# Reordering the products and the output parts in layer 0's attention loop of a two-layer gated cross-attention kernel

## The reference, cut to what matters

```python
# x: (8, 128, 512) float32, ctx_4096: (8, 128, 512), D=512, 32 heads of 128
x = x + jnp.tanh(g_xattn[0]) * _L0_xattn_ref(_layernorm(x), ctx_4096, mask, bias, ln_w, w_q, w_k, w_v, w_out)
x = x + jnp.tanh(g_ffn[0])   * _L0_ffn_ref(_layernorm(x), qweight, lut4, lut8, bias)      # dequantised weight
x = x + jnp.tanh(g_xattn[1]) * _L1_xattn_ref(_layernorm(x), ctx_4096, Wq, Wk, Wv, Wo, q_norm_w, k_norm_w)
x = x + jnp.tanh(g_ffn[1])   * _L1_ffn_ref(_layernorm(x), weight, bias)

# _L0_xattn_ref, with x = rmsnorm(hidden) * ln_w:
h_q = (x @ w_q.T); h_k = (kv @ w_k.T); h_v = (kv @ w_v.T)        # each split into 32 heads
score = softmax(where(mask, h_q h_k^T + bias, -inf)); score = where(mask, score, 0)
attn = score h_v                                                 # (b, q, 32*128)
out = attn @ w_out.T
return hidden_states + out
```

## Time and profile before

| | |
|---|---|
| median of 3 runs | 1681.61 us (1681.59 to 1682.12) |
| profiled execution, its own time | 1681.52 us |
| its span, first to last instruction | 1679.7 us |
| PE busy | 1663.4 us (99%) |
| DVE, ACT, POOL busy | 1190.1 (71%), 1001.6 (60%), 603.5 us (36%) |
| layer 0's loop | about 415.8 to 890 us of the span |

### The profile page before, as it was taken

One profiled execution on the slowest core, in us unless ns is written; L12 is line 12 of the kernel. 1 busy time (PEld: TensorE's weight loads), 2 busy tenths in 40 slices (PEclk: granted clock), 3 DMA queues, 4 the chain that ended last, 5 costly groups with the idle time before them and its releaser, 6 DMA issues.

```text
span 1679.7 us, 30969 instructions
## 1 busy us (share of the span) xinstructions
PE 1663.4 (99%) x10269; PEld 1477.9 (88%) x10269; DVE 1190.1 (71%) x2245; ACT 1001.6 (60%) x2540; POOL 603.5 (36%) x584
## 2 busy tenths in 40 slices
PE   9999999999999999999999999999999999999998
PEld 8899999999888888888888888888888888888887
DVE  6444446576787787777788877777676767677677
ACT  5344434345767777776776666656666665666563
POOL 2422223201434443534435543333333333333343
PEclk9999999999999999999999999999999999999999
DMA  6444444544233333333332110101010111111001
GB/s 227 175 167 157 150 150 150 192 165 161 95 106 102 112 112 99 126 100 120 108 113 83 39 51 24 63 26 59 12 62 25 52 32 50 36 36 41 14 7 51
DMA packets 80591, 153.31 MB, mean 91 GB/s; under 512 B 6544, under 2 KB 58128, under 8 KB 76944
## 3 DMA queue, kind: packets, MB, share of 16 engines
q1 hardware_dynamic: 80528, 152.50, 26.9%
HBM read 108.43 MB, written 44.04 MB: 91 GB/s over the span
## 4 chain that ended last, share of the span: by engine, by line
PE 87%; DVE 5%; ACT 3%; issue 3%; POOL 2%; DMA 1%; SPq 0%; ACTq 0%; POOLq 0%; DVEq 0%
PE bank L2103 20%; PE bank L2050 15%; PE bank L2052 15%; PE bank L2051 15%; PE bank L2280 7%; PE bank L2500 3%; PE bank L2238 3%; PE bank L2316 3%; PE bank L2400 2%; PE bank L2526 2%; PE bank L2226 1%; DMA vraw<-wv 1%; PE bank L2531 1%; ACT pr L1048 1%; PE bank L2072 0%
## 5 line engine op out<-in xcount | busy, mean ns | idle before, releaser
L2050 PE MATMUL bank<-w_hi,xt_hi 128*128 (+2 forms) x512 | 178.0, 348 | 1.2 <-DVE qt_lo L1949 1.1
L747 POOL TENSOR_TENSOR p<-p,rn 128x512 f32<-128x512 f32 x128 | 133.5, 1044 | 122.1 <-DVE rn L1917 118.8
L2052 PE MATMUL bank<-w_hi,xt_lo 128*128 (+2 forms) x512 | 172.7, 337 | 0.0
L2051 PE MATMUL bank<-w_lo,xt_hi 128*128 (+2 forms) x512 | 171.4, 335 | 0.0
L690 POOL TENSOR_TENSOR pr<-pr,rn 128x512 f32<-128x512 f32 x64 | 67.5, 1055 | 284.3 <-DVE rn L1564 284.3
L1203 ACT ACTIVATE p<-bank,nb,q_r 128x256 f32<-128x256 f32 x256 | 141.2, 562 | 3.3 <-DVE nb L1913 0.8
L609 POOL TENSOR_TENSOR q_r<-q_ms,half 128x4 f32<-128x4 f32 x64 | 64.4, 1007 | 190.6 <-DVE q_ms L1892 190.6
L1048 ACT ACTIVATE pr<-sc,nmax 128x128 f32<-128x128 f32 x256 | 99.9, 391 | 41.6 <-DVE nmax L1549 41.3
L609 POOL TENSOR_TENSOR k_r<-k_ms,half 128x2 f32<-128x2 f32 x64 | 59.3, 927 | 144.3 <-DVE k_ms L1871 144.3
L2050 PE MATMUL bank<-w_hi,ot_hi 128*128 (+1 forms) x256 | 106.2, 415 | 1.3 <-DVE ot_lo L1937 1.3
L2050 PEld LDWEIGHTS bank<-w_hi,xt_hi 128*128 128x128 f32 x512 | 96.2, 188 | 12.4 <-DVE qt_lo L1949 1.6
(11 more groups left out here) (293 smaller groups left out, 5605.2 us busy)
## 6 DMA issues: line engine op xcount, KB each, us to landing
stage<-w SPq DMA_DIRECT2D x35, 512.0 KB, 3.2
keys_of_layer<-kout SPq DMA_DIRECT2D x16, 1024.0 KB, 4.5
values_of_layer<-vout SPq DMA_DIRECT2D x16, 1024.0 KB, 5.2
kt<-keys_of_layer SPq DMA_DIRECT2D x64, 256.0 KB, 3.3
vs<-values_of_layer SPq DMA_DIRECT2D x64, 256.0 KB, 2.8
vraw<-wv SPq DMA_DIRECT2D x10, 1024.0 KB, 6.7
kraw<-wk SPq DMA_DIRECT2D x16, 512.0 KB, 5.6
stage0o<-w SPq DMA_DIRECT2D x16, 512.0 KB, 3.3
```

The costliest lines, as they stand in the source:

```text
L747: pool.tensor_tensor(p1[:, half_p:half_p + 2, :], p1[:, half_p:half_p + 2, :], rn1[:, half_p:half_p + 2].unsqueeze(2).to_broadcast([P, 2, ...
L2050: nc.tensor.matmul(out_ap, l_hi, r_hi, start=(c == 0), stop=False)
L2051: nc.tensor.matmul(out_ap, l_hi, r_lo, start=False, stop=False)
L2052: op = nc.tensor.matmul(out_ap, l_lo, r_hi, start=False, stop=(c == n - 1))
```

## The change

In layer 0's loop, from the last slot of turn 0 on:

- PE makes the output projection right behind the query products and the attention product at the end of the slot.
- ACT makes `output_hi` at the head of the next slot instead of late in its own.
- DVE makes `output_lo` at the head of the next slot, ahead of `maxima`, instead of behind `inverse_sums`.
- In turn 7, slots 4 to 7, PE's order stays; slot 4 now takes `output_hi` and `output_lo` at its head as slots 5 to 7 do already, and there DVE makes them ahead of `accumulate(i - 2)`.

No instruction is added or taken away.

```diff
--- before.py
+++ after.py
@@ -1067,8 +1067,7 @@
                 last = isinstance(t, int) and t == TL - 1
 
                 if last and j >= 4:
-                    if j > 4:
-                        output_hi(i - 1, j - 2)
+                    output_hi(i - 1, j - 2)
                     code_distance(t, j // 4, p, i + 1)
                     probabilities_copied(i)
                     code_mask(i + 1)
@@ -1078,6 +1077,8 @@
                     query_weight_late(n + 1)
                 if first and j == 1:
                     queries_out(3)
+                if not first:
+                    output_hi(i - 1, j - 2)
                 if not (first and j == 0):
                     probabilities_copied(i)
                 if first and j == 0:
@@ -1092,7 +1093,7 @@
                         queries_out(k + 1)
                 if not first:
                     query_part(n + 1, 1 - parity, p)
-                if not (first and j == 0):
+                if first and 0 < j < BODY - 1:
                     output_hi(i, j - 1)
                 if first and j == 3:
                     act.wait_ge(w_in[0], 48)
@@ -1689,10 +1690,9 @@
                 active = not first
 
                 if last and j >= 4:
+                    output_lo(i - 1, (j - 2) % 2)
                     if j == 4:
                         accumulate(i - 2, 2)
-                    else:
-                        output_lo(i - 1, (j - 2) % 2)
                     maxima(i + 1, j % 2)
                     if j == 4:
                         output_weight_lo(n, parity)
@@ -1719,7 +1721,7 @@
                 inverse_sums(i + 1, 2 * (j % 4))
                 if first and j == 1:
                     query_weight_lo(1, 2)
-                if lag1:
+                if first and 0 < j < BODY - 1:
                     output_lo(i, (j - 1) % 2)
                 if first:
                     behind_output(j)
@@ -2355,9 +2357,12 @@
                 if not (first and j == 0):
                     if not isinstance(t, int):
                         pe.wait_ge(v_in[(j - 1) % 2], 16 * (4 * t + (j + 1) // 2))
-                    attention_output(i, (j - 1) % 2)
+                    if first and j < BODY - 1:
+                        attention_output(i, (j - 1) % 2)
                 if not (first and j < 2):
                     output_projection(i - 1, (j - 2) % BODY, 2 * t + (j - 2) // 4)
+                if not (first and j < BODY - 1):
+                    attention_output(i, (j - 1) % 2)
 
             pe.wait_ge(c12_done, LAST_JOB)
             transpose_rows(0, 4)
```

## The result

| | before | after |
|---|---|---|
| median, five runs of each on one chip | 1681.75 us (1681.59 to 1682.81) | 1699.78 us (1695.98 to 1700.58) |
| ratio, with its 95% interval | | 1.0103 [1.0092, 1.0114] |
| profiled execution, its own time and span | 1681.52, 1679.7 | 1700.58, 1698.7 |

The change makes the kernel 1.0% slower.

The account below looks back on a forecast made before the run. The prediction took PE, busy 99% of the span, to bound the kernel. Its terms, 12.5 + 0.8 + 0.7 + 2.3 + 1.2 = 17.5 us on the profiled execution's 1681.5, gave 1699.0 us, range 1692.5 to 1704.5.

Parts of the forecast that it names:

- Term 1: Short slots: PE waits 0.90 us for YA's accumulation before the projection; 7.37 us against 6.36, over 13 slots +12.5.
- The head of turn 7: Slots 5 to 7 of turn 7, taken as model of the changed slot's head: accumulation starts 2.77 us after the scores.
- Term 2: Long slots: no wait, only passing between kinds of product; +0.02 us over 38 slots, +0.8 (-0.8 to +3).
- Term 3: First slot of each pair: ot_hi behind two weights, PE goes on at 4.15 against 4.13; +0.7 us (0 to +6.5).
- Term 4: Entry, slot 0 of turn 1: ot_hi late on ACT, slot takes 10.88 us; +2.3 (+1 to +3).
- Term 5: Exit, slot 4 of turn 7: projection at 2.31, slot 6.05 us against 4.99; +1.2 in all (0.5 to 2).
- (a): Rival: short slots' accumulation begins at 1.9 us or sooner, so PE does not wait; about 1681 us, chance 0.05.
- (b): Rival: ot_hi comes 0.7 us late in all slots, so long slots lose time too; 1716 us, chance 0.07.
- (c): Rival: DVE operations need a full flush between them, each step to the accumulation 1.1 us; 1755 us, chance 0.01.
- (d): Rival: the wait is only half as long, the accumulation having a shorter chain in front; about 1691 us, chance 0.07.
- the ring: Round through ACT and DVE, exponentials to nmax, each step waiting for the one before, one round a slot: 8.12 us.

Follow-up runs that it names:

- experiment 3: The changed kernel with one more DVE operation (low part of the early query weight) ahead of the accumulation in 12 short slots: 1706.95 us, ratio 1.0154.
- experiment 2: The changed kernel with PE's old order (attention product, then projection) in the short slots alone: 1692.54 us, ratio 1.0069.
- experiment 4: The changed kernel with DVE's accumulations of YA and YB moved ahead of ot_lo and the maxima at every slot's head: 1718.85 us, ratio 1.0226.
- experiment 5: The changed kernel with the accumulations ahead of ot_lo and the maxima, and wl cut from 512 to 64 columns: 1699.56 us in a single run.
- experiment 6: The changed kernel with both accumulations behind ot_lo but ahead of sc and nmax: 1736.71 us, ratio 1.0326.
- experiment 8: The kernel before with PE's new order of products alone, ACT and DVE as they were: 1800.47 us in a single run.
- experiment 1: The changed kernel with ACT's ot_hi ahead of qw_hi in the first slot of each pair of heads: 1696.52 us, ratio 1.0089.
- experiment 7: The changed kernel with only YA read out ahead of sc in short slots, and ot_hi ahead of qw_hi in each pair's first slot: 1693.05 us, ratio 1.0065.
- experiment 9: The changed kernel with PE's old order in short slots and ot_hi ahead of qw_hi in each pair's first slot: 1685.75 us, ratio 1.0024.

## Why the prediction was right, and where not

- **What bounds the kernel.** Right. PE sets the pace, and what the change costs are PE's waits. The reading that an order can win only in passing between kinds of product was borne out: attention product and projection take 0.89 + 2.74 = 3.63 in long slots, as before in the other order.
- **Term 1, short slots, +12.5.** Right in cause and size: 7.36 to 7.37 measured, 7.37 forecast. The head of turn 7 was the right model, and experiment 3 shows the cause: one more DVE operation ahead lengthens the wait by about its own length, 0.7 to 0.8 us.
- **Term 2, long slots, +0.8.** The slot grew by 0.007 instead of 0.02, so +0.3, nearer to nothing. Matmuls of 512 columns follow each other at 0.23 us in either order (in the change 494.38, 494.61).
- **Term 3, first slot of each pair, +0.7.** Nothing was lost: 7.767. The accumulation begins 3.16 after the scores there (3.29 was forecast) and ends 0.1 us before PE would wait; and these slots are 12, not 13. That it stands close to the edge was right; experiment 2 pushed it over, for 0.4 a pair.
- **Term 4, entry, +2.3.** Mis-sized: 3.8. The chain itself was right: the projection starts 490.41 - 483.30 = 7.11 after the scores, 7.14 was forecast. The step that failed is "7.14 + 2.85": after that wait the projection took 4.43, at a granted clock of 0.62 in the stretch. The text had priced every wait as idle time alone, and so the term left its own bounds of +1 to +3.
- **Term 5, exit, +1.2.** Right: +1.1, slot 4 at 6.06 where 6.05 was forecast.
- **The sum.** 17.5 forecast; 17.7 in the loop of the profiled execution, the terms' errors of +1.5, -0.5, -0.7 and -0.1 nearly cancelling. That the sum is this close is luck; that it is near is not, since term 1, which makes up most of it, came out slot by slot. The rest of that execution's 19.1 lies ahead of turn 1.
- **The rivals.** (a), no wait, fell: the accumulation starts at 2.76, not 1.9. (b) fell: long slots keep 7.767. What it described did appear in experiment 2, in one slot of four. (c) fell: DVE's starts stay 0.60 to 0.72 apart behind operations of 0.68. (d) fell: the chain ahead of the accumulation is as long as in turn 7.

What failed outright was the first repair (experiment 4). I read the wait as one late operation and moved it forward, without following what stood behind it round through ACT and back into DVE. Experiments 4 to 6 show that round trip by its length: outside the first slot of a pair, 0.45 us off wl took 0.46 or 0.47 off the way from nmax to nmax (8.12 to 7.66, 7.94 to 7.47), and accumulations on either side of ot_lo gave the same 8.12 and 7.94.

Left open: whether the 1.5 us ahead of turn 1 are scatter, as the other traces suggest; and why a wait of 2.7 us brings the clock down in one execution and not in another. Nor was it tried to free YA sooner with another bank.

## What to carry to other kernels

Before an operation is moved up on a waited-for engine, follow what it then delays, engine by engine, until the path comes back to its own queue: that round trip is a lower bound for the loop, and an operation inside it costs its full length even where both engines show idle time. Where two products can be made in either order, look at which of their inputs is made last; here swapping them gave PE nothing (7.767 against 7.760 us a slot) and brought the projection 0.81 us nearer to a read-out that was 0.26 us early, and that itself comes 0.2 us later with ot_lo ahead of it. And a long wait of PE may cost more than its length.

## What was not expected of the hardware

**A wait of PE can be paid twice.** The traces hold these waits in layer 0's loop, with what followed:

| idle time of PE | where | speed of the projection behind it |
|---|---|---|
| up to 1.7 us | all other waits for it in these traces | full, 0.23 us a matmul |
| 2.3 | experiment 8, turn 7 slot 4 | full |
| 2.3 | experiment 5, turn 7 slot 4 | half, projection 4.46 us |
| 2.5, 2.6 | experiment 8, the last short slot; experiment 6, turn 7 slot 4 | half, 4.34; half from the fifth matmul on, 4.26 |
| 2.7 | entry of the change and of experiment 2 | half, 0.43 us a matmul, 4.43 and 4.39 |
| 2.7, 2.9 | entry of experiment 3; experiment 4, turn 7 slot 4 | full |
| 3.4 | experiment 8, 12 short slots | half, 4.2 to 5.3 us, each time |

So behind waits of 2.3 to 2.9 us either speed followed, and 2.9 us were harmless where 2.3 were not. The half speed costs 1.3 to 2.4 us on a projection of 2.85. Of the five executions of the change four show a mean clock of 0.999 and one, at 1695.98 us, 1.000; that one is the fastest by 3.6 us, more than the half speed alone explains. In experiments 1, 7 and 9, where the profile shows no such wait over 1.7 us, all 20 executions counted above show 1.000. So in these runs the half speed came only where PE had waited 2.3 us or more, and there not always.

**A DVE operation on three operands makes hardly any headway beside POOL's bm.** Two rows of wl with nothing on POOL beside it, with 512 columns (experiment 8) and with 64 (experiment 5, turn 0):

```profile
610.17 0.75 DVE L1539 SCALAR_TENSOR_TENSOR wl<-eq,lut,wl 128x512 f32<-128x512 f32 x1 [0.20 <-ACT eq L1014]
```

```profile
430.49 0.28 DVE L1540 SCALAR_TENSOR_TENSOR wl<-eq,lut,wl 128x64 f32<-128x64 f32 x1 [1.52 <-ACT eq L1014]
```

In experiments 4 and 5 POOL's masked bias bm (L668) runs beside wl for 0.65 us of it, and wl takes 1.20 us with 512 columns and 0.73 to 0.75 with 64: 0.45 us more in both cases. With the change the two run together for 1.02 us in the last slot of a pair, and wl takes 1.57. So experiment 5 took off what 512 columns cost over 64 (0.75 - 0.28 = 0.47), and another 0.45 of the ring's wl are time beside bm. This is read from the times alone; no run moved bm.
